# Per-image convolution weights crossed by DMA, and SyncE's queue in another order

## The chip, the cores and the metric

The kernel runs on one core of one Trainium2 chip. The metric is the device time of one execution in microseconds (us), as the median of several runs. Engines: TensorE (PE), VectorE (DVE), ScalarE (ACT), GpSimd (POOL), SyncE (SP), which issues nearly all DMAs here.

## The reference

Sixteen images of 32 channels and 96 x 96 pixels. Each is normalised per channel; the pooled channel means choose a softmax mixture over seven expert kernels; with the two mixed 3 x 3 kernels the image goes through two convolutions, with a relu between them and two residual additions.

```python
identity = x                        # x here is _gn(x): each channel minus its mean, over its deviation
pooled = x.mean(axis=(-2, -1))
gate = jax.nn.softmax(pooled @ gate_w.T + gate_b)
kw1 = jnp.einsum('be,eoihw->boihw', gate, experts_w1) + conv1_w
kw2 = jnp.einsum('be,eoihw->boihw', gate, experts_w2) + conv2_w
out1 = jax.nn.relu(per_sample(x, kw1, kb1))
out2 = per_sample(out1, kw2, kb2)
return identity + out2 * RES_SCALE  # and the kernel's input is added once more
```

## The kernel before

**Layout.** An image lies in SBUF as 4 groups of 32 partitions, group g with the rows g, g+4, g+8 and so on (24 rows of 96 pixels per partition, `img`, 128 x 2304 float32, a ring of six). A 3 x 3 convolution needs rows of neighbouring groups. So every operand exists twice: "straight" (`a1`, `a2`) and "crossed" (`c1`, `c2`), the same with the two halves of the partitions exchanged. The weights too: `wts[i][STRAIGHT]` and `wts[i][CROSSED]`, three sets in turn. Everything is split into a high and a low float16 part, and the products are high x high, high x low, low x high.

**One image, in steps.** SP loads it (`load`, line 273, four DMAs of 288 KB). DVE makes its statistics (`statistics`, line 600), PE sums over the partitions of a channel (`gather_rows`, line 358), DVE and POOL make the coefficients. ACT writes the normalised image (`normalise`, `high_part`, lines 490 and 495), POOL the low part (`low_part`, line 858, signals `lo1_ok`). SP copies `a1` to `c1` with the halves exchanged (`cross1`, line 300, two DMAs of 588 KB, signals `crossed1`). DVE mixes the weights from the expert bank (`mixture`, line 645, seven operations), ACT rounds their high part (line 518), DVE subtracts the low part and copies both halves across (`weights`, lines 662 and 665, signals `w_ok`). PE convolves in five groups of rows (`conv1_group`); ACT applies the relu (`hidden`, line 533), DVE makes its low part (`hidden_low`, line 672), ACT crosses it (`cross2`, line 549), PE convolves again (`conv2_group`). DVE adds result and residual (`finish`, line 688, signals `fin_ok`), SP stores (`store`, line 287, eight DMAs: four of 180 KB after three groups, four of 108 KB after all five).

**Order.** No scheduler: each engine has a function `slot(s)` that lists its steps for image number s, with offsets, and `schedule` runs it: slots of the prologue unrolled, then a loop of two turns of six slots (images 2 to 13), then the rest unrolled. `run(step, s, offset, first)` makes the step for image s + offset, if that is at least `first`. Each engine works its own list in order, and waits on semaphores. For SP a slot is: load of image s+2, cross1 of image s, both halves of the store of image s-2. PE's slot is conv1 of image s, then conv2 of image s-1, with the gather matmul between the fourth and fifth group of conv1. The first group of conv1 waits for `w_ok` of the image, for `lo1_ok` and `crossed1` (`wait_low_part`), and for the first finish operation of image s-2, whose PSUM bank it takes.

**DVE's order** around the change: mixture, hidden_low of group 3, biases, weights (662, the two copies 665), hidden_low of group 4, clear_rim, finish 0 and 1, softmax_in, finish 2 and 3; then, in the next slot, finish 4 and the statistics of the image loaded last. DVE's `link` after an operation adds a semaphore step and waits for it; the loop counts seven links a slot.

Of the kernel before, what the change touches and what calls it, by code (L numbers as in the profile page):

```python
# [31 lines left out]
ALU = mybir.AluOpType  # L32
# [8 lines left out]
STRAIGHT, CROSSED = 0, 1  # L41
HI, LO = 0, 1
# [3 lines left out]
WSETS = 3  # L46
RING = 6
# [43 lines left out]
def build(nc, x, w1, b1, w2, b2, ew1, eb1, ew2, eb2, gw, gb, out):  # L91
    N, C, H, W = x.shape
    E = ew1.shape[0]
# [7 lines left out]
    TAPS = 3 * 2 * C  # L101
# [8 lines left out]
    with ctx:  # L110
# [3 lines left out]
        def sem(name):  # L114
            return ctx.enter_context(nc.semaphore(name))
# [13 lines left out]
        mix = sb("mix", [P, 2, 2, TAPS + 1])  # L129
        wts = [[sb(f"wts{i}_{k}", [P, 2, 2, TAPS], F16) for k in range(2)] for i in range(WSETS)]  # L130
# [60 lines left out]
        mix_ok = sem("mix_ok")  # L191
        whi_ok = sem("whi_ok")
        w_ok = sem("w_ok")
        res_ok = sem("res_ok")
        conv1_ps = sem("conv1_ps")
        hid_ok = sem("hid_ok")
# [17 lines left out]
        def halves(t):  # L214

            return t[0:P // 2], t[P // 2:P]
# [8 lines left out]
        def run(step, s, offset, first, *args):  # L225


            t = s.plus(offset)
            if not isinstance(t.i, int):
                assert t.c >= first and t.c + (LAPS - 1) * RING < N  # L230
                step(t, *args)
            elif first <= t.number < N:
                step(t, *args)

        def schedule(slot, eng, begin, first, last, link=None, per_slot=0):


            for s in range(begin, first):
                slot(Sample(0, s))
            start = link.n if link else 0  # L240
            with eng.Fori(0, LAPS) as i:
                if link:
                    link.base, link.n = i * (per_slot * RING) + start, 0
                for c in range(RING):
                    slot(Sample(i, first + c))
                if link:
                    assert link.n == per_slot * RING, link.n
            if link:
                link.base, link.n = start + per_slot * RING * LAPS, 0
            for s in range(first + RING * LAPS, last + 1):  # L250
                slot(Sample(0, s))
# [4 lines left out]
        @block.sync  # L256
        def _(sp):
            xv = x.rearrange("n c (k g) w -> n g c k w", g=G)
            ov = out.rearrange("n c (k g) w -> n g c k w", g=G)

            def load(t):
                if early(t):

                    for arrived, b0 in ((x_half[t.ring], 0), (x_in[t.ring], NB // 2)):
                        for g in range(G):
                            sp.dma_start(img[t.ring][g * C:(g + 1) * C, b0:b0 + NB // 2, :],
                                         xv[t.number, g, :, b0:b0 + NB // 2, :]).then_inc(arrived, 16)
                    return
                if not isinstance(t.i, int) or t.at_least(RING):

                    sp.wait_ge(stored[t.ring], STORE * (t.lap + 1))
                for g in range(G):
                    sp.dma_start(img[t.ring][g * C:(g + 1) * C, :, :],  # L273
                                 xv[t.number, g]).then_inc(x_in[t.ring], 16)

            def store(t, half):


                if t.known(N - 1):
                    pieces = (((0, 2), (2, 3)), ((3, 4), (4, GRP)))[half]  # L280
                else:
                    pieces = (((0, 3),), ((3, GRP),))[half]
                for g0, g1 in pieces:
                    b0, b1 = g0 * SPG, min(g1 * SPG, NB)
                    sp.wait_ge(fin_ok, t.number * GRP + g1)
                    for g in range(G):
                        sp.dma_start(ov[t.number, g, :, b0:b1, :],  # L287
                                     img[t.ring][g * C:(g + 1) * C, b0:b1, :]).then_inc(stored[t.ring], 16)

            def cross1(t):  # L290


                if early(t):
                    parts = ((hi1_ok, HI, LO, crossed1_high[t.ring]), (lo1_ok, LO, 2, crossed1[t.ring]))
                else:
                    parts = ((lo1_ok, HI, 2, crossed1[t.ring]),)
                for ready, p0, p1, done in parts:
                    sp.wait_ge(ready, t.number + 1)
                    for half, d0 in ((0, 0), (1, 1)):
                        sp.dma_start(halves(c1[t.parity])[half][:, p0:p1, d0:d0 + NB, :].rearrange("p a b w -> p a (b w)"),  # L300
                                     halves(a1[t.parity])[half][:, p0:p1].rearrange("p a b w -> p a (b w)")
                                     ).then_inc(done, 16)

            load(Sample(0, 0))

            def slot(s):
                run(load, s, 2, 1)
                run(cross1, s, 0, 0)
                run(store, s, -2, 0, 0)
                run(store, s, -2, 0, 1)  # L310

            schedule(slot, sp, -2, 2, 17)
            for b in range(RING):
                images = len(range(b, N, RING)) + (2 if b == (N - 1) % RING else 1)
                sp.wait_ge(stored[b], STORE * images)
# [3 lines left out]
        def _(pe):  # L319
# [69 lines left out]
            def conv1_group(s, g):  # L389
                if g == 0:  # L390

                    pe.wait_ge(w_ok, s.number + 1)
                    if early(s):
                        pe.wait_ge(crossed1_high[s.ring], 32)
                    else:
                        wait_low_part(s)

                if s.at_least(2):
                    pe.wait_ge(fin_ok, (s.number - 2) * GRP + g + 1)
                else:  # L400
                    pe.wait_ge(hid_ok, g + 1)
                products(0, s, g, PRODUCTS, *conv1_sides(s, g)).then_inc(conv1_ps, 1)

            def first_conv1():

                s = Sample(0, 0)
                pe.wait_ge(w_ok, 1)
                pe.wait_ge(crossed1_high[0], 32)
                pe.wait_ge(wt_act, 4)
                pe.wait_ge(wt_dve, 4)  # L410
                for g in range(GRP):
                    products(0, s, g, PRODUCTS[:2], *conv1_sides(s, g))
                for g in range(GRP):
                    products(0, s, g, PRODUCTS[2:], *conv1_sides(s, g)).then_inc(conv1_ps, 1)
# [171 lines left out]
        def _(dve):  # L586
# [4 lines left out]
            def statistics(t):  # L591
                if early(t):
                    dve.wait_ge(x_half[t.ring], LOAD)
                else:
                    dve.wait_ge(x_in[t.ring], LOAD * (t.lap + 1))
                flat = img[t.ring][:, :, :].rearrange("p b w -> p (b w)")
                for j in range(STAT):
                    if early(t) and j == STAT // 2:
                        dve.wait_ge(x_in[t.ring], LOAD)
                    last = nc.vector.bn_stats(stats[t.ring][:, j, :], flat[:, j * SC:(j + 1) * SC])  # L600
                link(last)
# [28 lines left out]
            def softmax_out(t):  # L630

                c = col[t.ring]
                dve.wait_ge(expo_ok, t.number + 1)
                link(nc.vector.reciprocal(c[:, RSUM:RSUM + 1], c[:, ESUM:ESUM + 1]))
                link(nc.vector.tensor_scalar(gate[t.ring][:, 0:E], expo[t.ring][:, :], c[:, RSUM:RSUM + 1], None,
                                             ALU.mult))
# [21 lines left out]
            def weights(t):  # L658

                dve.wait_ge(whi_ok, t.number + 1)  # L660
                st, cr = wts[t.c % WSETS][STRAIGHT], wts[t.c % WSETS][CROSSED]
                link(nc.vector.tensor_tensor(st[:, :, LO, :], mix[:, E % 2, :, 0:TAPS], st[:, :, HI, :],  # L662
                                             ALU.subtract))
                for a, b in ((0, 1), (1, 0)):
                    last = nc.vector.tensor_copy(halves(cr)[a].rearrange("p v a b -> p (v a b)"),  # L665
                                                 halves(st)[b].rearrange("p v a b -> p (v a b)"))
                last.then_inc(w_ok, 1)

            def hidden_low(s, g):
                dve.wait_ge(hid_ok, s.number * GRP + g + 1)  # L670
# [89 lines left out]
            biases(Sample(0, 0))  # L760
            softmax_in(Sample(0, 1))
            weights(Sample(0, 0))
            softmax_out(Sample(0, 1))
            for e in range(E):
                mixture(Sample(0, 1), e)
            biases(Sample(0, 1))
            weights(Sample(0, 1))
            statistics(Sample(0, 2))
            aggregate(Sample(0, 2))
            hidden_low(Sample(0, 0), 0)  # L770
# [35 lines left out]
                run(finish, s, -1, 0, 2)  # L806
                run(finish, s, -1, 0, 3)

            schedule(slot, dve, 1, 2, 17, link, 7)


        @block.gpsimd
# [99 lines left out]
```

## Time and profile before

| | us |
|---|---|
| median of 3 runs | 372.83 |
| the runs | 371.85, 372.83, 376.41 |
| the profiled execution | 373.65 |
| its span, first to last instruction | 371.8 |
| PE busy | 320.5 |
| DVE busy | 301.0 |

The profile is of one execution. Its span leaves out 1.85 us that lie around the instructions. "Busy" of PE is modelled and not its peak rate. The program is the same for every image once the prologue is over, so a slot (the time from one image's conv1 to the next one's) is what is compared. In the rows, L375 is PE's product in the helper `products`, which both convolutions use; `c<-a` of line 300 on SPq is the DMA that crosses the image, `c<-a` of line 549 on ACT is cross2.

### The profile page before, as it was taken

Reading aid. Unit: us, or ns where it says so; the run is one execution under the profiler, and the core shown is the slowest. Engines: PE = TensorE matmul, PEld = TensorE weight load, DVE = VectorE, ACT = ScalarE, POOL = GpSimd, SP = SyncE. Lnnn points to the kernel's source line nnn. Section 1 sums busy time; section 2 is a strip of 40 time slices with the busy share of each in tenths; the row PEclk is TensorE's granted clock in tenths of the full one; section 3 lists DMA queues with packets and bytes.
Section 4 is the critical chain, followed back from the end, with each engine's and each line's share of the span. In section 5 each row is a group of like instructions: output and inputs, shape, how many; then the busy total and the mean of one; then the engine's idle time right before and its main releaser. Section 6 shows DMA issues by size and latency. Waiting matters only on the chain.

```text
span 371.8 us, 8541 instructions
## 1 busy us (share of the span) xinstructions
PE 320.5 (86%) x2983; PEld 198.4 (53%) x2983; DVE 301.0 (81%) x679; ACT 252.6 (68%) x278; POOL 199.6 (54%) x236
## 2 busy tenths in 40 slices
PE   2328773599999997999997999989999999999994
PEld 2216532356465754565554557555556555676552
DVE  3699945699979998899988799998999898796432
ACT  1155229877877887797877578887778787866720
POOL 8039417492928484666648084847576674933000
PEclk9999968599999999999999899999999999999999
DMA  9942990607989596949795795969697967194055
GB/s 194 219 74 56 229 189 2 130 3 189 198 191 194 136 234 151 219 116 220 168 203 127 175 194 150 220 150 230 147 203 165 213 148 178 42 216 112 18 130 127
DMA packets 107148, 58.19 MB, mean 157 GB/s; under 512 B 102497, under 2 KB 103009, under 8 KB 107105
## 3 DMA queue, kind: packets, MB, share of 16 engines
q1 hardware_dynamic: 106304, 57.03, 72.3%
q10 hardware_dynamic: 608, 0.59, 0.6%
q8 instruction: 26, 0.43, 0.5%
q14 instruction: 18, 0.14, 0.1%
q0 software_dynamic: 192, 0.01, 0.0%
HBM read 19.47 MB, written 18.87 MB: 103 GB/s over the span
## 4 chain that ended last, share of the span: by engine, by line
PE 38%; DVE 26%; DMA 11%; issue 9%; SPq 9%; ACT 3%; POOL 2%; ACTq 0%; DVEq 0%; POOLq 0%
PE pg L375 36%; DMA c<-a 10%; DVE mix L645 6%; DVE a L672 5%; DVE img L688 4%; SPq L273 4%; SPq L287 3%; DVE wts L662 3%; DVE stats L600 2%; SPq L300 2%; PE pg L338 2%; POOL a L858 1%; DMA natural<-in_L_conv_conv_w 1%; PE pstat L358 1%; DVE wts L665 1%
## 5 line engine op out<-in xcount | busy, mean ns | idle before, releaser
L375 PE MATMUL pg<-a,wts 128*64 128x480 f16 (+1 forms) x1440 | 295.2, 364 | 15.1 <-DMA c<-a 9.2
L375 PE MATMUL pg<-c,wts 128*64 128x480 f16 (+1 forms) x1440 | 300.7, 369 | 0.0
L375 PEld LDWEIGHTS pg<-c,wts 128*64 128x64 f16 x1440 | 155.3, 110 | 72.6 <-issue 1.1
L375 PEld LDWEIGHTS pg<-a,wts 128*64 128x64 f16 x1440 | 155.8, 110 | 52.1 <-issue 15.3
L858 POOL TENSOR_TENSOR a<-xh,a 128x576 f16<-128x576 f32 x64 | 85.3, 1364 | 12.9 <-POOL col L866 8.5
L533 ACT ACTIVATE hid<-pg,col 128x480 f32<-128x480 f32 x80 | 52.4, 656 | 40.8 <-PE pg L375 26.1
L549 ACT COPY c<-a 64x2352 f32<-64x2352 f32 x32 | 68.9, 2153 | 16.3 <-DVE a L672 13.2
L645 DVE SCALAR_TENSOR_TENSOR mix<-bank,gate,mix 128x386 f32<-128x386 f32 x96 | 74.0, 771 | 2.4
L839 POOL TENSOR_TENSOR col<-col,minus_half 128x1 f32<-128x1 f32 x16 | 13.5, 845 | 113.6 <-DVE col L618 113.6
L672 DVE TENSOR_TENSOR a<-hid,a 128x480 f16<-128x480 f32 x80 | 55.5, 695 | 20.8 <-ACT a L533 19.1
L872 POOL TENSOR_SCALAR img<-img,col 128x1152 f32<-128x1152 f32 x32 | 58.4, 1834 | 0.1
L688 DVE SCALAR_TENSOR_TENSOR img<-pg,img 128x480 f32<-128x480 f32 (+1 forms) x80 | 47.1, 631 | 12.7 <-PE pg L375 10.2
L533 ACT ACTIVATE a<-pg,col 128x480 f16<-128x480 f32 x80 | 52.6, 657 | 0.0
L600 DVE BATCH_NORM_STATS2 stats<-img 128x6 f32<-128x384 f32 x96 | 45.6, 544 | 0.1
L490 ACT ACTIVATE xh<-img,col 128x2304 f32<-128x2304 f32 x16 | 36.9, 2306 | 10.0 <-POOL col L840 10.0
L495 ACT ACTIVATE a<-img,col 128x2304 f16<-128x2304 f32 (+1 forms) x17 | 37.3, 2194 | 6.5 <-POOL col L840 6.5
L662 DVE TENSOR_TENSOR wts<-mix,wts 128x384 f16<-128x384 f32 x16 | 20.6, 1290 | 0.3 <-ACT wts L518 0.3
L358 PE MATMUL pstat<-triples,same 128*128 128x12 f32 x32 | 6.9, 290 | 15.4 <-DVE triples L607 15.4
L518 ACT CAST wts<-mix 128x384 f16<-128x384 f32 x16 | 8.2, 512 | 16.0 <-DVE mix L645 16.0
L358 PEld LDWEIGHTS pstat<-triples,same 128*128 128x128 f32 x32 | 5.4, 211 | 21.4 <-DVE triples L607 16.0
L665 DVE COPY wts<-wts 64x768 f16<-64x768 f16 x32 | 13.2, 414 | 0.8
L615 DVE COPY col<-pstat 128x1 f32<-128x1 f32 x16 | 2.5, 157 | 13.3 <-PE pstat L358 13.0
(61 smaller groups left out, 146.0 us busy)
## 6 DMA issues: line engine op xcount, KB each, us to landing
c<-a SPq DMA_DIRECT2D x28, 588.0 KB, 8.7
img<-in_x SPq DMA_DIRECT2D x56, 288.0 KB, 5.6
out<-img SPq DMA_DIRECT2D x60, 180.0 KB, 3.0
out<-img SPq DMA_DIRECT2D x60, 108.0 KB, 2.4
c<-a SPq DMA_DIRECT2D x8, 294.0 KB, 5.3
img<-in_x SPq DMA_DIRECT2D x16, 144.0 KB, 5.0
out<-img SPq DMA_DIRECT2D x4, 120.0 KB, 2.1
out<-img SPq DMA_DIRECT2D x8, 60.0 KB, 1.8
```

Of the source, the lines that this page charges most:

```text
L375: last = nc.tensor.matmul(pg[g][side * 64:side * 64 + 64, at:at + nb * W].rearrange("p (b w) -> p b w", w=W), wts[s.c % WSETS][kind][:, v, ...
L490: nc.scalar.activation(xh[t.parity][:, :, :], img[t.ring][:, :, :], ACT.Identity, bias=c[:, NBIAS:NBIAS + 1], scale=c[:, RSTD:RSTD + 1]).t ...
L495: return nc.scalar.activation(a1[t.parity][:, HI, b0:b1, 1:1 + W], img[t.ring][:, b0:b1, :], ACT.Identity, bias=c[:, NBIAS:NBIAS + 1], sca ...
L533: last = nc.scalar.activation(o, pg[g][:, 0:SPG * W].rearrange("p (b w) -> p b w", w=W), ACT.Relu, bias=c[:, B1:B1 + 1], scale=HS / WS)
L549: last = nc.scalar.copy(d, a[:, :, first:first + NB * RP // 2])
L600: last = nc.vector.bn_stats(stats[t.ring][:, j, :], flat[:, j * SC:(j + 1) * SC])
L645: nc.vector.scalar_tensor_tensor(out=mix[:, (e + 1) % 2, :, :], in0=bank[:, e, :, :], scalar=gate[t.ring][:, e:e + 1], in1=bank[:, E, :, : ...
L662: link(nc.vector.tensor_tensor(st[:, :, LO, :], mix[:, E % 2, :, 0:TAPS], st[:, :, HI, :], ALU.subtract))
L672: nc.vector.tensor_tensor(a2[s.parity][:, LO, j0:j1, 1:1 + W], hid[g_parity(s, g)][:, :, :], a2[s.parity][:, HI, j0:j1, 1:1 + W], ALU.subt ...
L688: nc.vector.scalar_tensor_tensor(out=r, in0=pg[g][:, 0:(b1 - b0) * W].rearrange("p (b w) -> p b w", w=W), scalar=1.0 / (WS * HS), in1=r, o ...
L858: last = nc.gpsimd.tensor_tensor(a1[t.parity][:, LO, b0:b1, 1:1 + W], xh[t.parity][:, b0:b1, :], a1[t.parity][:, HI, b0:b1, 1:1 + W], ALU. ...
L872: last = nc.gpsimd.tensor_scalar(img[t.ring][:, b0:b1, :], img[t.ring][:, b0:b1, :], c[:, RS1:RS1 + 1], c[:, RB:RB + 1], ALU.mult, ALU.add)
```

## The change

- DVE's two copies (line 665) leave `weights`; `w_ok` now comes right after the subtraction of line 662, without a link. For images 0 and 1 the copies are still made on DVE (`cross_early`, right behind `weights`).
- For images 2 and on SP makes the copies as two DMAs of 96 KB (`cross_weights`), after a wait for `w_ok`; a new semaphore per ring place, `w_crossed`, is what PE waits for.
- SP's slot becomes: load of image s+2, cross_weights of image s, both halves of the store of image s-2, cross1 of image s+1. So the sequence of the steady part was store(s-2), load(s+3), cross1(s+1), store(s-1), and is now store(s-2), cross1(s+1), load(s+3), cross_weights(s+1), store(s-1). In the prologue, load 4 moves from ahead of cross1 of image 2 to behind it.
- DVE's loop counts six links a slot.

```diff
             load(Sample(0, 0))
+            load(Sample(0, 1))
+            load(Sample(0, 2))
+            cross1(Sample(0, 0))
+            load(Sample(0, 3))
+            cross1(Sample(0, 1))
 
             def slot(s):
-                run(load, s, 2, 1)
-                run(cross1, s, 0, 0)
+                run(load, s, 2, 4)
+                run(cross_weights, s, 0, 2)
                 run(store, s, -2, 0, 0)
                 run(store, s, -2, 0, 1)
-
-            schedule(slot, sp, -2, 2, 17)
+                run(cross1, s, 1, 2)
+
+            schedule(slot, sp, 1, 2, 17)
...
+            def cross_weights(t):
+
+                sp.wait_ge(w_ok, t.number + 1)
+                st, cr = wts[t.c % WSETS][STRAIGHT], wts[t.c % WSETS][CROSSED]
+                for a, b in ((0, 1), (1, 0)):
+                    sp.dma_start(halves(cr)[a].rearrange("p v a b -> p (v a b)"),
+                                 halves(st)[b].rearrange("p v a b -> p (v a b)")).then_inc(w_crossed[t.ring], 16)
...
-                    pe.wait_ge(w_ok, s.number + 1)
+                    pe.wait_ge(w_crossed[s.ring], 32 * (s.lap + 1))
...
-                link(nc.vector.tensor_tensor(st[:, :, LO, :], mix[:, E % 2, :, 0:TAPS], st[:, :, HI, :],
-                                             ALU.subtract))
+                nc.vector.tensor_tensor(st[:, :, LO, :], mix[:, E % 2, :, 0:TAPS], st[:, :, HI, :],
+                                        ALU.subtract).then_inc(w_ok, 1)
+
+            def cross_early(t):
+                dve.wait_ge(w_ok, t.number + 1)
+                st, cr = wts[t.c % WSETS][STRAIGHT], wts[t.c % WSETS][CROSSED]
                 for a, b in ((0, 1), (1, 0)):
                     last = nc.vector.tensor_copy(halves(cr)[a].rearrange("p v a b -> p (v a b)"),
                                                  halves(st)[b].rearrange("p v a b -> p (v a b)"))
-                last.then_inc(w_ok, 1)
+                last.then_inc(w_crossed[t.ring], 32)
```

## Rows read from the trace of the kernel before

**Rows 1.** The page: busy us, share of the span, instructions, of each engine
```profile
PE 320.5 (86%) x2983; PEld 198.4 (53%) x2983; DVE 301.0 (81%) x679; ACT 252.6 (68%) x278; POOL 199.6 (54%) x236
```

**Rows 2.** Waits of PE at line 375: us in total, times, longest us
```profile
PE pg L375 <- DMA c<-a: 9.2, 5, 5.2
...
PE pg L375 <- DVE img L688: 5.5, 4, 2.3
```

**Rows 3.** Timeline of PE, first product of conv1: start, us, [idle before <- releaser]
```profile
103.13 0.34 PE L375 MATMUL pg<-a,wts 128*64 128x384 f16 x1 [1.64 <-DVE img L688]
...
143.26 0.32 PE L375 MATMUL pg<-a,wts 128*64 128x384 f16 x1 [2.18 <-DMA c<-a]
...
181.95 0.32 PE L375 MATMUL pg<-a,wts 128*64 128x384 f16 x1 [0.75 <-DMA c<-a]
...
203.27 0.52 PE L375 MATMUL pg<-a,wts 128*64 128x384 f16 x1 [2.25 <-DVE img L688]
```

**Rows 4.** Timeline of PE, gather matmul: images 4, 5, 6 and 15
```profile
89.88 0.39 PE L358 MATMUL pstat<-triples,same 128*128 128x12 f32 x2
...
110.59 0.39 PE L358 MATMUL pstat<-triples,same 128*128 128x12 f32 x2
...
129.47 0.39 PE L358 MATMUL pstat<-triples,same 128*128 128x12 f32 x2
...
310.23 0.39 PE L358 MATMUL pstat<-triples,same 128*128 128x12 f32 x2
```

**Rows 5.** Timeline of SP, one slot: start of the first issue, us of issuing
```profile
162.73 5.17 SPq L287 DMA_DIRECT2D out<-img  x8
168.10 2.96 SPq L273 DMA_DIRECT2D img<-in_x  x4
171.11 1.87 SPq L300 DMA_DIRECT2D c<-a  x2
```

**Rows 6.** Chain that ended last, same slot: start, us (issue to landing), what
```profile
172.34 9.37 DMA c<-a
```

**Rows 7.** Windows: us, busy per engine, PEclk, DMA share, GB/s; loads moving
```profile
170.00:175.00 5.00, 5.00 (x50) 2.74 (x52) 4.79 (x11) 4.38 (x5) 4.12 (x7) 1.00 1.22 236
```

**Rows 8.** Timeline of DVE, same slot: copies, last hidden_low, finish 2 to 4
```profile
158.88 0.72 DVE L665 COPY wts<-wts 64x768 f16<-64x768 f16 x2
159.64 0.66 DVE L672 TENSOR_TENSOR a<-hid,a 128x480 f16<-128x480 f32 x1
...
162.05 1.68 DVE L688 SCALAR_TENSOR_TENSOR img<-pg,img 128x480 f32<-128x480 f32 x3
```

**Rows 9.** SP's stores, then line 300, in a slot without loads: issues and landings
```profile
302.50 4.83 SPq L287 DMA_DIRECT2D out<-img  x8
...
L300 SPq DMA_DIRECT2D c<-a x2: 600/600/600, 307.5 to 308.2; - x2
...
DMA to landing us min/median/max: 5.3/6.7/8.1
```

**Rows 10.** Timelines of POOL (low_part) and of DVE (hidden_low behind low_part's start)
```profile
159.67 5.34 POOL L858 TENSOR_TENSOR a<-xh,a 128x576 f16<-128x576 f32 x4 [0.77 <-POOL col L866]
...
79.17 1.74 DVE L672 TENSOR_TENSOR a<-hid,a 128x480 f16<-128x480 f32 x1
```

**Rows 11.** Lines 300 and 273 in the prologue, loads issued behind crossings: issues, landings
```profile
L300 SPq DMA_DIRECT2D c<-a x2: 881/968/1056, 43.0 to 43.9; - x2
...
DMA to landing us min/median/max: 6.8/7.2/7.5
...
L273 SPq DMA_DIRECT2D img<-in_x x2: 564/2274/3985, 46.9 to 47.7; - x2
...
DMA to landing us min/median/max: 8.2/8.4/8.5
```

**Rows 12.** Timeline of DVE: statistics of the image loaded from 168.10 on
```profile
182.53 0.55 DVE L600 BATCH_NORM_STATS2 stats<-img 128x6 f32<-128x384 f32 x1
```

**Rows 13.** The page, DMA issues: count, KB each, median us to landing
```profile
out<-img SPq DMA_DIRECT2D x60, 108.0 KB, 2.4
```

More of the change, by code:

```diff
@@ L193, in build @@
         w_ok = sem("w_ok")
+        w_crossed = [sem(f"w_crossed{i}") for i in range(RING)]
         res_ok = sem("res_ok")
@@ L406, in first_conv1 @@
                 s = Sample(0, 0)
-                pe.wait_ge(w_ok, 1)
+                pe.wait_ge(w_crossed[0], 32)
                 pe.wait_ge(crossed1_high[0], 32)
@@ L762, in _ @@
             weights(Sample(0, 0))
+            cross_early(Sample(0, 0))
             softmax_out(Sample(0, 1))
@@ L767, in _ @@
             weights(Sample(0, 1))
+            cross_early(Sample(0, 1))
             statistics(Sample(0, 2))
@@ L807, in slot @@
                 run(finish, s, -1, 0, 3)
-            schedule(slot, dve, 1, 2, 17, link, 7)
+            schedule(slot, dve, 1, 2, 17, link, 6)
         @block.gpsimd
```

## Prediction

> **What bounds the kernel now.** I read the page first: TensorE (PE) is busy 86% of a span of 371.8 us, no other engine more than 81% [rows 1]. So the question is where PE stands still. Its waits [rows 2] name two causes for its product line L375: the DMA c<-a (9.2 us, five times) and DVE's img (5.5 us, four times). The timeline of PE shows where: each time it is the first product of conv1 of an image [rows 3]. The longest of the five, 5.2 us, is conv1 of image 1 in the prologue; the 2.25 us at 203.27 are conv1 of image 8, where the loop turns (two turns of six images from image 2 on). That leaves 9.2 - 5.2 + 5.5 - 2.25 = 7.2 us in seven stalls of the steady part. Three of them are put down to img; I count them as the same stall, since conv1's first group waits for the crossing too, and of the finish operations only for the first, which is done before the others that the profile may name.
>
> The gather matmul of line 358 runs once an image, 7.46 us after conv1 starts, and is the clock for a slot [rows 4]: 129.47 - 110.59 = 18.88 us for a slot without stall, 110.59 - 89.88 = 20.71 for one with the stall of 1.64, so a stall costs its length and 0.19 more. From 89.88 to 310.23 are 11 slots, 220.35 us. At 18.88 they would be 207.7; 7.2 + 7 x 0.19 = 8.5 of the difference are the seven stalls, the rest (4.1) is the turn of the loop and stays. **8.5 us is all that this change can win in the steady part.**
>
> Why does PE stall? Through SP's queue [rows 5]: stores from 162.73, loads from 168.10, crossing from 171.11. The crossing's second DMA is issued at 172.34 and lands 9.37 us later, and PE starts conv1 0.24 us behind that, at 181.95 [rows 3, 6]. It is slow because it stands behind the loads on the same transfer engines, which are full: 1.22 mean busy share while the loads move [rows 7]. So there is a loop of two parts. Call C the start of conv1 and S the start of the stores: a = from C of one image to S in the next slot, b = from S to C of the slot after. From [rows 3, 5]: a = 162.73 - 143.26 = 19.47, b = 181.95 - 162.73 = 19.22, together 38.69 for two slots. The pair before took 143.26 - 103.13 = 40.13. Mean over the 11 slots without the 4.1: 19.66.
>
> **The change, part by part.**
>
> *The copies go.* Two DVE copies, 0.72 us together [rows 8], once an image. Behind them stand the last hidden_low, clear_rim and the finish operations, one behind the other with no idle time until the third finish, which releases the stores. So S comes 0.72 earlier: a = 18.75 instead of 19.47. For images 0 and 1 the copies stay (cross_early); the prologue keeps its time.
>
> *The crossing c<-a goes ahead of the loads.* The slot at 302.50 has no loads, so it shows the new order [rows 9]: stores issued at 302.50, crossing from 307.54, second DMA issued at 308.15 and landed 8.1 later, at 316.3: S + 13.8, against S + 19.0 now (181.71 - 162.73). It is then 5 us early for PE, and is off the path. Its input is ready: low_part of that image ran from 159.67 to 165.01 [rows 10], the crossing is issued at about 168.
>
> *The loads go last.* The one place where loads were issued behind crossings is the prologue [rows 11]: the last crossing was issued at 43.9 and landed 7.5 later, at 51.4, the last load was issued at 47.7 and landed 8.5 later, at 56.2. So loads end 4.8 us behind the crossing: S + 18.6. Who wants them? statistics of that image, one slot on, at 182.53 in the trace, which is S + 19.8 [rows 12]; 1.2 us to spare, and DVE's next appointment is the gather, 7 us on. I cost this at nothing; if a load is later, DVE waits the difference. In the prologue load 4 now stands behind cross1 of image 2, which waits for POOL's low_part; its statistics come only in the next slot, behind the first image's finish operations, so I cost that at nothing too.
>
> *The weights' crossing.* Two DMAs of 96 KB each, 28 in all, and SP waits for w_ok in front of them, with the next stores queued behind. w_ok comes at 158.85, which is C + 15.6; the stores are due at C + 18.75, and two issues take some 1.2 (0.6 each) [rows 9], so the stores are not held. The trace of before has no such DMA. Bounds: from below, nothing shorter than the 0.72 of the copies is plausible; the nearest row is the store of 108 KB, 2.4 us from issue to landing, of which the issue spacing is 0.6 [rows 13]; from above, the crossing of 588 KB without loads, 8.1 [rows 9]. In a quiet queue, by the nearest row: w_ok + 0.6 for the second issue + 2.4 = C + 18.6, against PE's arrival at C + 18.88. That just fits. But the queue isn't quiet: the loads end at S + 18.6, and the weights (192 KB, a sixth of the 1,152 KB that take 4.8 to 5.0 us) follow in 0.9 us. Landed: S + 19.5. With the 0.25 until PE runs, b = 19.75.
>
> The Trainium skill (DMA: Bandwidth & Descriptors, section Rules for kernel authors) speaks against this part: two transfers to disjoint partition halves serialise, since both use the same 16 engines. Its page SBUF — State Buffer (section The DMA setup-cost knee) gives about 2 us plus size over 436 GB/s, so an estimate of 2.2 us for 96 KB, three times the copies; with the second issue it gives C + 18.4 in a quiet queue, by which the sum would not change.
>
> **The sum.** a + b = 18.75 + 19.75 = 38.5, or 19.25 a slot, against 19.66 now: 0.41 x 11 = 4.5 us less. The profiled execution took 373.65 (span 371.8 and 1.85 around it), 0.8 above the median of 372.83. So 369.1 by its own measure, 368.3 by the median. I say **368.3 us**. The tail behind the last load (from 310.23 on) has no stall to lose.
>
> **The rivals.**
>
> *Nothing binds any more* (chance 0.22). If loads and weights together end 0.8 us earlier than I add up (the loads' HBM reads may already run while the crossing moves), b + a falls to 37.8 and PE's own 18.88 is the floor: 8.5 us less, 364.3. For it: 1.22 in [rows 7] shows that packets of the two kinds overlap. Against it: in [rows 11] they could overlap as well and still took 4.8.
>
> *DVE gives the 0.72 back* (0.14). The last hidden_low reads two SBUF tiles, like POOL's low_part. In [rows 8, 10] it starts 0.03 ahead of low_part (159.64 against 159.67) and takes 0.66; at 79.17 it took 1.74, which I read as low_part having come first. POOL's low_part began only when the copies ended, so without them both start together again, 0.72 earlier. If POOL wins each time, a = 18.75 + 1.08 = 19.83, 19.79 a slot: 0.13 x 11 = 1.4 us more, 374.2. The Trainium skill (SBUF — State Buffer, section Who interferes with whom) states the lock behind it: of the two engines one has the shared port pair for a whole instruction. The trace agrees (1.74 against 0.66).
>
> *The small transfer becomes the new wait, and the kernel slower* (0.14). The place is PE's wait for w_crossed. If the weights add more than 1.7 us behind the loads instead of 0.9, a + b passes 39.3 and nothing is won; with 3.0, which is the 2.4 of the 108 KB row counted from the loads' landing and one issue more, b = 21.85, 20.3 a slot, 0.64 x 11 = 7 us more: 380. For it: SP waits for w_ok and can't issue earlier. Against: both DMAs are issued 3 us before the loads have landed, so their start-up is hidden.
>
> **How the numbers follow.** Forecast 0.50, spread 366 to 371; rivals as above. The range reaches from the floor of 364.3, less half a microsecond of noise, to the middle of the slower case: 363.8 to 376.5; outside remain about 0.05 below and 0.1 above. Faster by over 2% means below 365.4, slower means above 380.3 (2% is about what a measurement of this kernel can tell from no change): faster takes nearly all of the first rival and the low end of the forecast, 0.24; slower only the end of the last, 0.06; within 2%, 0.70.
>
> **What would show it.** Right: no PE wait on c<-a after 100 us; c<-a from issue to landing about 7 to 8 us; gather to gather 18.9 to 19.4; the remaining stalls of PE ended by wts<-wts, landing 0.5 to 1 us behind the last load; stores 0.7 us earlier behind w_ok. Wrong: statistics waiting for img<-in_x by more than 1 us in most slots, hidden_low at 1.74 in most slots, or weights landing more than 1.7 us behind the loads.

## Result

| | median us | ratio to before | 95% interval |
|---|---|---|---|
| before | 374.68 (16 runs) | | |
| changed kernel | 370.64 (16 runs, 369.81 to 372.27) | 0.990 | 0.9875 to 0.9925 |

The changed kernel is 1% faster: about 3.7 us by the ratio, 4.0 between the two medians. 368.3 us, 4.5 less than before, was forecast; more runs of the kernel before moved its median up from 372.83. By ratio the forecast was 0.988.

The profiled execution took 372.14 us (span 370.3). Its waits of PE (us in total, times, longest) no longer have the seven stalls behind the image crossing that the prediction counted in [rows 2]; the two left on c<-a lie in the prologue. In their place stands the new transfer:

```profile
PE pg L390 <- DMA c<-a: 6.0, 2, 5.2
PE pg L390 <- DMA wts<-wts: 5.7, 6, 1.9
PE pg L390 <- issue: 3.5, 2, 1.9
```

The timeline of PE after, first products of conv1 that stand behind a wait (compare [rows 3]). The last two lie at the turn of the loop:

```profile
101.99 0.34 PE L390 MATMUL pg<-a,wts 128*64 128x384 f16 x1 [0.52 <-DMA wts<-wts]
...
141.18 0.35 PE L390 MATMUL pg<-a,wts 128*64 128x384 f16 x1 [1.24 <-DMA wts<-wts]
...
181.07 0.35 PE L390 MATMUL pg<-a,wts 128*64 128x384 f16 x1 [1.95 <-DMA wts<-wts]
...
202.00 0.34 PE L390 MATMUL pg<-a,wts 128*64 128x384 f16 x1 [1.87 <-issue]
...
205.71 0.39 PE L390 MATMUL pg<-a,wts 128*64 128x480 f16 x1 [1.68 <-issue]
```

And the gather matmul of images 4, 5, 6 and 15 (compare [rows 4]):

```profile
89.87 0.39 PE L373 MATMUL pstat<-triples,same 128*128 128x12 f32 x2
...
109.46 0.39 PE L373 MATMUL pstat<-triples,same 128*128 128x12 f32 x2
...
128.33 0.39 PE L373 MATMUL pstat<-triples,same 128*128 128x12 f32 x2
...
308.25 0.39 PE L373 MATMUL pstat<-triples,same 128*128 128x12 f32 x2
```

Eleven slots take 218.38 us instead of 220.35. So the stalls of the steady part went from 7.2 to 5.7 us, and not to nothing. This one execution gained 2 us there; its 372.14 is at the upper end of the runs of the changed kernel, and the one profiled before (373.65) was below its median, so the two profiles show less than the medians do.

One slot of SP after (compare [rows 5]), then issue and landing of the second crossing DMA (L301), of the last load (L274) and of the two weight DMAs (L310):

```profile
120.73 5.26 SPq L288 DMA_DIRECT2D out<-img  x8
126.04 1.30 SPq L301 DMA_DIRECT2D c<-a  x2
127.54 6.90 SPq L274 DMA_DIRECT2D img<-in_x  x4
136.49 1.17 SPq L310 DMA_DIRECT2D wts<-wts  x2
...
L301 SPq DMA_DIRECT2D c<-a x2: 610/624/638, 126.0 to 126.7; - x2
...
DMA to landing us min/median/max: 5.4/6.5/7.7
...
L274 SPq DMA_DIRECT2D img<-in_x x1: 827/827/827, 133.6 to 133.6; - x1
...
DMA to landing us min/median/max: 7.0/7.0/7.0
...
L310 SPq DMA_DIRECT2D wts<-wts x2: 532/564/597, 136.5 to 137.1; - x2
...
DMA to landing us min/median/max: 3.4/3.7/4.1
```

The crossing lands at 126.7 + 7.7 = 134.4, the last load at 133.6 + 7.0 = 140.6, the weights at 141.1, and PE starts at 141.18. In all six slots that stall on them, the weights land 0.3 to 0.6 us behind the last load. The chain that ended last says the same of this slot:

```profile
136.49 0.53 SPq L310
137.02 0.04 issue
137.06 4.07 DMA wts<-wts
141.13 0.04 issue
141.18 0.84 PE pg L390 x7
```

### The profile page after: what moved, and what is told of

Its sections match the earlier page's. It is cut to its first block, busy times and chain, and to the rows that moved or that the text cites. A ratio compares the mean times of both kernels' runs of the same rounds, so it can differ in the third digit from the quotient of the medians.

```text
span 370.3 us, 8529 instructions
## 1 busy us (share of the span) xinstructions
PE 317.8 (86%) x2983; PEld 199.9 (54%) x2983; DVE 288.6 (78%) x651; ACT 252.7 (68%) x278; POOL 192.8 (52%) x236
## 3 DMA queue, kind: packets, MB, share of 16 engines
HBM read 19.47 MB, written 18.87 MB: 104 GB/s over the span
## 4 chain that ended last, share of the span: by engine, by line
PE 59%; DVE 15%; DMA 9%; issue 7%; SPq 3%; ACT 3%; POOL 2%; ACTq 0%; DVEq 0%; POOLq 0%
PE pg L390 56%; DMA wts<-wts 6%; DVE mix L660 5%; DVE wts L677 3%; DVE a L691 2%; DMA c<-a 2%; PE pg L353 2%; DVE stats L615 2%; PE pstat L373 2%; POOL a L879 1%; SPq L274 1%; DMA natural<-in_L_conv_conv_w 1%; SPq L310 1%; DVE img L707 1%; SPq L301 1%
## 5 line engine op out<-in xcount | busy, mean ns | idle before, releaser
L879 POOL TENSOR_TENSOR a<-xh,a 128x576 f16<-128x576 f32 x64 | 79.0, 1267 | 13.0 <-POOL col L887 8.5
L691 DVE TENSOR_TENSOR a<-hid,a 128x480 f16<-128x480 f32 x80 | 52.5, 657 | 23.1 <-ACT a L548 22.3
L707 DVE SCALAR_TENSOR_TENSOR img<-pg,img 128x480 f32<-128x480 f32 (+1 forms) x80 | 48.1, 633 | 15.4 <-PE pg L390 13.1
L353 PE MATMUL pg<-ident,padded 128*128 128x128 f32 x24 | 5.6, 424 | 8.7 <-DVE padded L721 8.7
```

What stands on the lines that cost most here:

```text
L691: nc.vector.tensor_tensor(a2[s.parity][:, LO, j0:j1, 1:1 + W], hid[g_parity(s, g)][:, :, :], a2[s.parity][:, HI, j0:j1, 1:1 + W], ALU.subt ...
L707: nc.vector.scalar_tensor_tensor(out=r, in0=pg[g][:, 0:(b1 - b0) * W].rearrange("p (b w) -> p b w", w=W), scalar=1.0 / (WS * HS), in1=r, o ...
L879: last = nc.gpsimd.tensor_tensor(a1[t.parity][:, LO, b0:b1, 1:1 + W], xh[t.parity][:, b0:b1, :], a1[t.parity][:, HI, b0:b1, 1:1 + W], ALU. ...
```

## Experiments

In the text below, a is the time from conv1's start to the stores one slot on, b from there to the conv1 after, S the start of the stores, as in the prediction. Each experiment was timed against the kernel before in the same batch of runs; of the kernel with small loads there is one run. Diffs are cut to the lines that matter, and "..." marks what is left out.

### The order alone

```diff
 # the kernel before, SP only
+            load(Sample(0, 1))
+            load(Sample(0, 2))
+            cross1(Sample(0, 0))
+            load(Sample(0, 3))
+            cross1(Sample(0, 1))

             def slot(s):
-                run(load, s, 2, 1)
-                run(cross1, s, 0, 0)
+                run(load, s, 2, 4)
                 run(store, s, -2, 0, 0)
                 run(store, s, -2, 0, 1)
-
-            schedule(slot, sp, -2, 2, 17)
+                run(cross1, s, 1, 2)
+
+            schedule(slot, sp, 1, 2, 17)
```

> The kernel before with SP's new order alone: crossing of the next image right behind the stores, loads behind it; DVE keeps both copies, no DMA for the weights. Theory (two parts in a loop, a from conv1 to the stores one slot on, b from the stores to the conv1 after): the crossing lands at S + 13.5 to 14 and is off the path; no weights stand behind the loads, so nothing makes PE wait, and a slot is PE's own 18.88 us: 7 to 8.5 us less than before, ratio about 0.98, and so 3 to 5 us faster than the whole change. Loads land at about S + 20, just when DVE wants them (S + 20.3 with the copies still there); DVE may wait some tenths. Rival (both parts of the change are needed, since the copies delay the stores by 0.72 a slot): the loads land late, DVE waits, and the ratio is that of the whole change, 0.99, or worse.

Measured: 364.56 us, ratio 0.973 (0.968 to 0.977). That is 6 us faster than the whole change. Its gather matmuls:

```profile
91.51 0.39 PE L363 MATMUL pstat<-triples,same 128*128 128x12 f32 x2
110.38 0.39 PE L363 MATMUL pstat<-triples,same 128*128 128x12 f32 x2
129.26 0.39 PE L363 MATMUL pstat<-triples,same 128*128 128x12 f32 x2
148.14 0.39 PE L363 MATMUL pstat<-triples,same 128*128 128x12 f32 x2
...
303.18 0.39 PE L363 MATMUL pstat<-triples,same 128*128 128x12 f32 x2
```

Every slot but the one with the turn of the loop is 18.87 or 18.88 us; 303.18 - 91.51 = 211.67 = 11 x 18.88 + 4.0. No slot but that one holds a stall of PE: PE is the bound. The loads still arrive in time: in the slot whose stores start at 141.40 the last was issued at 153.8 and landed 6.5 later, at 160.2, and DVE took up its statistics at 161.06. The rival, that the copies would spoil it, falls.

The ratio says about 10 us (8.7 to 11.8), the slots of the profiled execution 8.7. That execution (366.63 us) was the slowest of its six, and its gather of image 4 comes 1.6 us later than before (91.51 against 89.88), in the prologue. Where the ratio's surplus lies is open.

### The weights' DMA alone

```diff
 # the changed kernel, SP only
-                run(load, s, 2, 4)
-                run(cross_weights, s, 0, 2)
-                run(store, s, -2, 0, 0)
-                run(store, s, -2, 0, 1)
-                run(cross1, s, 1, 2)
+                run(load, s, 2, 1)
+                run(cross1, s, 0, 0)
+                run(cross_weights, s, 0, 2)
+                run(store, s, -2, 0, 0)
+                run(store, s, -2, 0, 1)
...
```

The prologue has its old order too.

> The whole change but with SP's old order: load, image crossing, weights' crossing, stores. Theory: a falls by 0.72 as in the whole change, the image crossing still lands at S + 19 to 20, and the weights land about 0.5 behind it, so b grows by 0.5: (-0.72 + 0.5)/2 = -0.1 us a slot, 1 us less in 11 slots, ratio 0.995 to 1.00. PE's waits at conv1 are ended by wts<-wts. Rival (the gain of the change comes from the copies that left DVE, not from the order): ratio 0.99 as the whole change.

Measured: 374.73 us, ratio 1.000 (0.997 to 1.003), the top of what was expected. PE's waits (us, times, longest):

```profile
PE pg L385 <- DMA wts<-wts: 7.6, 6, 1.6
```

So the two parts of the change pull apart: the order is worth 2.7%, the weights' DMA nothing by itself, and the two together 1%.

### The copies gone and nothing in their place

```diff
 # the kernel before, weights() on DVE
...
+                if not (isinstance(t.i, int) and t.number < WSETS):
+                    low.then_inc(w_ok, 1)
+                    return
...
```

`low` is the subtraction of line 662; the crossed weights of images 0 to 2 are used again for the others.

> The kernel before without the two copies from image 3 on (left out, no DMA in their place: the crossed weights of images 0 to 2 are used again, so part of the computation is left out). SP's order is the old one. Theory: stores start 0.72 earlier behind the weights, a falls from 19.47 to 18.75, b stays, so each slot that is bound by the loop gets 0.36 us shorter: 3 to 4 us less, ratio 0.990 to 0.992. Rival (the copies are hidden behind other waits): ratio 1.00.

Measured: 370.68 us, ratio 0.989 (0.985 to 0.992), as the loop of a and b says: 0.36 us in each of 11 slots. (In the profiled execution the 11 slots took 217.35 us, 3.0 less.) Under the old order, then, the copies did cost about 4 us, and the DMAs that replace them give all of it back.

### The whole change without the transfers

```diff
 # the changed kernel
-                run(cross_weights, s, 0, 2)
...
-                    pe.wait_ge(w_crossed[s.ring], 32 * (s.lap + 1))
+                    pe.wait_ge(w_ok, s.number + 1)
...
```

DVE makes the crossed weights of images 0 to 2, which are used again for the others.

> The whole change without the weights' DMAs: crossed weights are made on DVE for images 0, 1 and 2 and used again for the others, so part of the computation is left out. SP's order is the new one, DVE has no copies in the loop. Theory: PE-bound, every slot 18.88 us, as with the new order and the copies: ratio 0.970 to 0.977; so the two small transfers alone cost what lies between this and the whole change, 5 to 6 us. The copies off DVE bring nothing once the order is new. Rival (the copies matter as well): faster than the order alone by 1% or more.

Measured: 366.31 us, ratio 0.977 (0.973 to 0.982). Within the intervals this is the order alone; it isn't faster. All slots but the one with the turn are 18.87 or 18.88 us, as with the order alone, so under the new order DVE's copies cost nothing in a slot, and the two small transfers cost about 1.3%.

The totals of these two kernels compare less well than their slots. In the profiled executions the slot with the turn took 25.55 us here and 22.90 with the order alone. PE stood at the turn about as long in both (2.32 and 1.43 us here, 2.31 and 1.33 there), but here the clock granted to it then fell to 0.50 (1.2 of 2.4 GHz) from 200 to 206 us, and there it stayed at 1.00. The page's rows of the clock, in tenths, each slice 9.1 us; the order alone first:

```profile
PEclk9955969689999999999999999999999999999998
...
PEclk9999989599999999999999799999999999999998
```

Why it fell in one and not in the other is not known. The order alone, in turn, loses the 1.6 us in the prologue; its clock was lower there (the third and fourth digit), and whether that is the reason is open.

### The transfer doubled

```diff
 # the changed kernel, cross_weights
+                for a, b in ((0, 1), (1, 0)):
+                    sp.dma_start(halves(spare[t.parity])[a].rearrange("p v a b -> p (v a b)"),
+                                 halves(st)[b].rearrange("p v a b -> p (v a b)")).then_inc(w_crossed[t.ring], 16)
...
```

PE waits for all four DMAs.

> The whole change with the weights' transfer doubled: two further DMAs of 96 KB into a spare tile, and PE waits for all four. Theory (the loop of a and b with the weights at its end): b grows by 0.9 for the bytes, or by 1.2 where the two further issues set it, so 0.5 to 0.6 us a slot, 5 to 7 us more than the whole change, ratio to before 1.00 to 1.01. Rival (only the last transfer's fixed latency counts, the bytes hide behind the loads): 1 us or less more, ratio 0.99.

Measured: 377.91 us, ratio 1.011 (1.007 to 1.015), 2.1% more than the whole change where 5 to 7 us (1.4 to 1.9%) were expected. PE now stands at every conv1, for instance:

```profile
122.36 0.35 PE L394 MATMUL pg<-a,wts 128*64 128x384 f16 x1 [0.64 <-DMA spare<-wts]
...
142.66 0.35 PE L394 MATMUL pg<-a,wts 128*64 128x384 f16 x1 [1.23 <-DMA spare<-wts]
...
162.57 0.32 PE L394 MATMUL pg<-a,wts 128*64 128x384 f16 x1 [0.85 <-DMA spare<-wts]
```

The page's row for the two further DMAs:

```profile
spare<-wts SPq DMA_DIRECT2D x28, 96.0 KB, 2.2
```

No transfer, one, two: 0.977, 0.990, 1.011. But the second pair does not wait for the loads as the first does in the changed kernel. In nine of the eleven slots from 102.66 on the last DMA lands 2.2 to 2.3 us behind its own issue, the same as in a quiet queue, and 1 to 3.7 us behind the last load. What sets PE's start is then a chain within one slot: w_ok at C + 15.6, four issues (the last one 1.9 us on, in two slots 2.7 to 2.9), 2.2 to land, 0.14 until PE runs, together 19.8; the slots without the turn average 19.9. So this run shows that what is added behind w_ok lies on the path, by its issues and its latency, and not what more bytes behind the loads cost. Which step is the larger is open: the ratios say the second, the slots of the profiled executions without the turn (18.88, 19.5, 19.9) the first.

### Small loads in front of the weights

```diff
 # the changed kernel, load
+                rows = NB if t.ring >= 4 or (isinstance(t.i, int) and t.number < 4) else NB // 2
...
-                    sp.dma_start(img[t.ring][g * C:(g + 1) * C, :, :],
-                                 xv[t.number, g]).then_inc(x_in[t.ring], 16)
+                    sp.dma_start(img[t.ring][g * C:(g + 1) * C, 0:rows, :],
+                                 xv[t.number, g, :, 0:rows, :]).then_inc(x_in[t.ring], 16)
```

> The whole change with half-size loads (144 KB instead of 288 KB, half of the rows left out) for 8 of the 12 images that the loop loads: images 6 to 9 and 12 to 15; images 4, 5, 10, 11 are loaded whole. So one execution holds both kinds. Theory (PE waits because the weights stand behind the loads): in the slots whose loads are half-size (conv1 of images 5 to 8 and 11 to 13 follows them) the weights land 2.5 us or less after issue, at C + 18.4, and gather to gather is 18.88; where the loads are whole PE still waits 0.4 us or more. Rival (the weights' own latency is what PE waits for): the slots stay at 19.1 or more with half-size loads too.

Measured: 366.87 us, in a single run. The weights' DMAs of one slot with small loads, issue and landing, and PE's waits on them in the whole execution:

```profile
L311 SPq DMA_DIRECT2D wts<-wts x2: 496/546/597, 135.1 to 135.7; - x2
...
DMA to landing us min/median/max: 2.1/2.1/2.1
...
PE pg L391 <- DMA wts<-wts: 0.4, 1, 0.4
```

2.1 us instead of 3.4 to 4.1: in a quiet queue the transfer fits. All slots behind the first are 18.88 us, but for the one with the turn (24.82 us, with the granted clock at 0.50 again).

The expectation placed the whole loads one slot too late. In SP's list load s+2 stands ahead of the weights of image s, so the weights of images 2, 3, 8 and 9 stand behind whole loads (images 4, 5, 10 and 11), all others behind half ones. Behind image 3's, PE's wait is the one of 0.4 us above, at 100.63: the last load landed at 100.01, the weights 0.5 later, after 3.1 us, and the slot is 19.45 us. Image 2 did not wait for them, image 8 is the turn, and image 9 did not stall in the changed kernel either, behind a turn that had let all transfers finish early (the loads at 214.5 here, the weights at 219.3). So the one whole load that could show a stall did, by about the 0.4 us expected, and none of the half ones did. What delays the weights is what stands in front of them, not their own latency. It is one run, and only one slot carries the whole-load side.

### The weights on another queue

```diff
 # the changed kernel: cross_weights issued by ACT
...
                 run(high_part, s, 2, 2)
+                run(cross_weights, s, 1, 2)
...
```

> The whole change, but the two DMAs of the weights are issued by ACT, behind high_part, on ACT's own DMA queue and so not behind the loads of SP's queue. Theory (what is left of PE's waits is the weights standing behind the loads in one queue): they land 2 to 3 us after issue also while loads move, at C + 19.0 or earlier (issue at about C + 16.4 behind high_part), PE's waits on wts<-wts fall below 0.3 us each, 2 to 4 us less than the whole change, ratio to before about 0.98. Rival (the 16 transfer engines are simply full, whatever the queue): the weights still land 0.4 to 1 us after the last load or the loads get later by as much, and the ratio stays 0.99. ACT's issues cost it about 1.2 us a slot ahead of cross2, which has room.

Measured: 371.37 us, ratio 0.990 (0.985 to 0.995): the rival was right. The page's row for the DMA, and two waits, of PE and of DVE for a late load:

```profile
wts<-wts ACTq DMA_DIRECT2D x28, 96.0 KB, 2.7
...
PE pg L381 <- DMA wts<-wts: 4.1, 5, 1.4
...
139.63 0.56 DVE L615 BATCH_NORM_STATS2 stats<-img 128x6 f32<-128x384 f32 x1 [0.32 <-DMA img<-in_x]
```

Median 2.7 us from issue to landing, against 2.6 on SP's queue. Both medians take slots with and without loads in front together; in the slot where PE starts at 140.14 the last load landed at 139.61 and the weights, issued at 135.77, at 140.10. In all five slots where PE waits for them they land 0.3 to 0.5 us behind the last load, as on SP's queue. A queue of its own does not take them past the loads. The Trainium skill says why (DMA: Bandwidth & Descriptors, section Issuing engines are not separate DMA queues): all issuers share the same 16 DMA engines, and another issuer saves only sequencer time. These runs agree: 0.990 on either queue. My expectation went against that rule.

### The order alone, with the loop written out

```diff
 # the order alone, schedule(), all engines
-            with eng.Fori(0, LAPS) as i:
...
-                for c in range(RING):
-                    slot(Sample(i, first + c))
...
+            for s in range(first, first + RING * LAPS):
+                slot(Sample(0, s))
```

> The new order with the copies on DVE, and the loop of two turns of six slots written out, on all engines. Of the 11 slots between the gathers of images 4 and 15, 4.0 us were put down to the turn of the loop. Theory: they go, all 11 slots are 18.88 us, ratio 0.960 to 0.965. Rival (what looked like the turn is instruction fetch, which a longer program needs all along): stalls of 1 to 2 us of PE appear in other places, ended by nothing that the profile shows, and the ratio is that of the order alone, 0.973, or worse.

Measured: 360.99 us, ratio 0.964 (0.959 to 0.968), the fastest kernel here. The gathers of images 4 and 15:

```profile
90.23 0.39 PE L356 MATMUL pstat<-triples,same 128*128 128x12 f32 x2
...
297.87 0.39 PE L356 MATMUL pstat<-triples,same 128*128 128x12 f32 x2
```

207.64 us, 11 times 18.88. What the prediction called the turn of the loop was that, and no stall took its place.

## Why the prediction was right, and where it was off

**The ceiling.** 8.5 us were said to be all that the steady part holds. With the order alone the 11 slots went from 220.35 to 211.67, 8.7 us less, and the rest of 4.0 us was the turn of the loop, as the unrolled kernel shows. Right, as is the reading that all seven stalls were the crossing's.

**The copies go, a = 18.75.** Conv1 at 101.99, stores at 120.73: 18.74. Right. The copies-gone run gives its worth under the old order (1.1%).

**The image crossing off the path, S + 13.8.** 134.4 - 120.73 = 13.7, and no stall of PE behind the prologue ends with c<-a. Right.

**Loads 4.8 us behind the crossing.** This is the term that was mis-sized. In the slot shown it is 140.6 - 134.4 = 6.2; over the slots of images 3 to 13 it is 4.8 to 6.5, mean 5.8, and 6.1 in the six that stall. The 4.8 came from one case in the prologue [rows 11].

**Weights 0.9 behind the loads.** 141.1 - 140.6 = 0.5, and 0.3 to 0.6 in the six slots that stall. Right in kind, less in size; the prediction's own figures, a sixth of 4.8 to 5.0, make 0.8. That part of the weights moves before the last load is in would explain the rest, and is not shown.

**b = 19.75.** From the stores at 120.73 to the conv1 at 141.18 it is 20.45: 13.7 + 6.2 + 0.5 and 0.05 until PE runs, where 0.25 were assumed. So a + b = 39.2 for this pair, not 38.5; b was 19.8 to 21.3 in the six slots. With the turn taken out (1.87 + 1.68 and the 0.19 of each), the 11 slots average (218.38 - 3.9)/11 = 19.5 against 19.25 forecast and 19.66 before. In that execution the gain was less than half of the forecast one, over all runs it was 3.7 of 4.5 us; why the medians differ by more than the profiles is not settled, but for where the profiled executions lie among the runs. The mechanism is shown; that the median came this close to the sum is in part luck, since the two mis-sized terms lean opposite ways and the profiled slots gained less than half of what was summed.

**The rivals.** "Nothing binds any more" is what the order alone does; the change does not reach it since the weights, not the loads' lateness for DVE, end the loop. "DVE gives the 0.72 back" did not come: hidden_low takes 0.65, and POOL's low_part begins when it is over:

```profile
136.38 0.65 DVE L691 TENSOR_TENSOR a<-hid,a 128x480 f16<-128x480 f32 x1
...
137.28 2.45 POOL L879 TENSOR_TENSOR a<-xh,a 128x576 f16<-128x576 f32 x2 [0.77 <-POOL col L887]
```

The rival misread [rows 10]. It took low_part's start for something that the copies' end lets go, and so expected both to move 0.72 earlier together. But both rows name POOL's own operation on `col` as what low_part waited for, 0.77 us behind it in either kernel, and low_part begins 0.82 us behind the weights' subtraction in both (137.28 and 136.46 here; 159.67 and 158.85 before). It is POOL's own list that sets it. Only hidden_low moved earlier, into the gap. Before, hidden_low began 0.03 ahead of low_part, and low_part's first operation took 1.73 us (the one at 299.45) where it now takes 1.24 (239.17). Over the whole execution low_part, before and after, fell by 6.3 us:

```profile
L858 POOL TENSOR_TENSOR a<-xh,a 128x576 f16<-128x576 f32 x64 | 85.3, 1364 | 12.9 <-POOL col L866 8.5
...
L879 POOL TENSOR_TENSOR a<-xh,a 128x576 f16<-128x576 f32 x64 | 79.0, 1267 | 13.0 <-POOL col L887 8.5
```

That agrees with one of the two engines holding the other up where they meet; no run tried it by itself.

"The small transfer becomes the new wait" came half true. It is the new wait, with the place that was named, but with 0.5 us behind the loads instead of the 1.7 that decide. The forecast and this rival are one mechanism at two sizes. The doubled transfer is slower than before, but mostly by another way, issues and latency behind w_ok.

**What the prediction missed** was not a term but a comparison. It summed both parts of the change and never asked what the order would do alone. With its own figures: a = 19.47, the crossing at S + 13.8, nothing behind the loads that PE needs. That makes 33.3 for two slots, under PE's own 37.8, so the loop is no longer closed by a DMA and 18.88 is the floor. The better kernel stood in the prediction's numbers.

## What to carry to other kernels

When a change has two parts that act on one loop, cost each by itself as well as both: here the one took the last transfer off the path, the other put a new one there. Work that an engine does in 0.7 us of its own time is not made free by a DMA if the transfer engines are the busy resource and the result is needed at the end of their queue; look at their busy share in the microseconds just ahead of the need, not at the mean. And order a queue by who waits: what the bounding engine needs goes first, what is wanted a slot later goes last.

## What the hardware showed beside that

- Four load issues took 2.96 us of SP [rows 5] when they stood behind stores, and 6.90 us when two crossings of 588 KB were still moving in front of them. That SP holds an issue back while much is outstanding is a reading that no run tested. It cost nothing here, because SP had nothing else to do until w_ok at 136.5, but these 4 us on the issuing engine appear in no row as a wait.
- The turn of the hand-written loop costs about 4 us once: with the order alone, two stalls of PE of 2.31 and 1.33 us at a granted clock of 1.00. Where the granted clock then fell to 0.50, it was 6.7 us (the change without the transfers). Written out, the stalls are gone, and 12 slots of straight code brought no new one.
- A DMA of 96 KB within SBUF took 2.1 us from issue to landing in a quiet queue, 3.4 to 4.1 with loads in front in the slot shown.
